# Latent attention scores: two products of 128 rows per head against three of 64, two heads in the two halves of the array

## What is computed

```python
H, DH, LAT = 16, 128, 64
q = (x @ W_q).reshape(B, S, H, DH).transpose(0, 2, 1, 3)
latent = x @ W_kv_down                                    # B, S, 64
kv = (latent @ W_kv_up).reshape(B, S, H, DH).transpose(0, 2, 1, 3)
scores = jnp.einsum('bhqd,bhkd->bhqk', q, kv) / np.sqrt(DH)
probs = jax.nn.softmax(scores, axis=-1)
out = jnp.einsum('bhqk,bhkd->bhqd', probs, kv)
return out.transpose(0, 2, 1, 3).reshape(B, S, H * DH) @ W_o
```

## Time and profile before

| | us |
|---|---|
| time, median of 3 runs | 1693.83 (1692.1 to 1697.16) |
| span of the profiled execution | 1695.7 |
| PE busy over the span | 1441.4 (85%) |
| DVE busy | 1075.4 (63%) |
| ACT busy | 750.3 (44%) |
| POOL busy | 773.8 (46%) |
| all score products (L2131, L2132), busy | 226.5 in 512 records |
| latent attention, first to last score product | 1156.9 to 1539.9 |

### The profile page before, as it was taken

The page is one execution under the profiler, slowest core; times in us unless marked ns, Lnnn a source line. Parts: engine busy times, 40 slices in busy tenths (PEclk is TensorE's granted clock), DMA queues, the critical chain, the costliest instruction groups (busy, mean ns, idle before and its releaser), DMA issues. The chain is left out here.

```text
span 1695.7 us, 39494 instructions
## 1 busy us (share of the span) xinstructions
PE 1441.4 (85%) x14334; PEld 990.9 (58%) x14334; DVE 1075.4 (63%) x2743; ACT 750.3 (44%) x1786; POOL 773.8 (46%) x741
## 2 busy tenths in 40 slices
PE   6879999448889996888999478877899999998799
PEld 3556656414545554455566356654677777777687
DVE  6852222457876564783222388876998888874888
ACT  5533333254555633553333311125776666752322
POOL 4453332763320000454333466606998888973000
PEclk9989999569999998899999788888999999999899
DMA  8309995631110002514999232200000000000000
GB/s 265 98 14 267 284 266 150 204 96 38 38 38 1 1 1 67 152 40 123 280 296 259 73 87 84 78 4 13 3 16 3 12 7 3 16 3 3 10 19 22
DMA packets 92664, 145.50 MB, mean 86 GB/s; under 512 B 25032, under 2 KB 52528, under 8 KB 92512
## 3 DMA queue, kind: packets, MB, share of 16 engines
q1 hardware_dynamic: 62816, 93.06, 19.1%
q0 software_dynamic: 15360, 37.77, 7.7%
q10 hardware_dynamic: 14336, 12.59, 2.7%
HBM read 122.39 MB, written 18.87 MB: 83 GB/s over the span
## 5 line engine op out<-in xcount | busy, mean ns | idle before, releaser
L2298 POOL TENSOR_TENSOR sb_m_prob<-sb_m_prob,sb_m_rinv 128x512 f32<-128x512 f32 x256 | 260.1, 1041 | 44.6 <-DVE sb_m_rinv L2348 40.8
L1272 POOL DMA_INDIRECT sb_c_rows<-slot_rows,sb_slot x192 | 192.1, 1000 | 102.7 <-issue 51.2
L2228 ACT ACTIVATE sb_m_prob<-m_ps_s,sb_m_nmax 128x512 f32<-128x512 f32 x256 | 173.8, 683 | 125.8 <-DVE sb_m_nmax L2354 125.2
L1106 POOL DMA_INDIRECT e_xn<-xn_rows,sb_table x128 | 117.7, 920 | 209.6 <-PE e_ps_x L1184 197.2
L1255 DVE TENSOR_TENSOR sb_e_h<-sb_e_sg,e_ps_gu 96x176 f32<-96x176 f32 x128 | 42.6, 333 | 256.5 <-ACT sb_e_sg L1231 256.5
L1193 PE MATMUL e_ps_gu<-e_wgu,sb_e_xT 128*96 128x352 f32 x512 | 178.1, 470 | 17.0 <-ACT sb_e_xT L1225 15.6
L2354 DVE TENSOR_REDUCE sb_m_nmax<-m_ps_s 128x1 f32<-128x512 f32 x256 | 163.8, 681 | 28.1 <-PE m_ps_s L2132 25.7
L2362 DVE STREAM_TRANSPOSE sb_m_pT<-sb_m_prob 128x1024 f32<-128x1024 f32 x128 | 157.5, 1232 | 0.0
L2145 PE MATMUL m_ps_v<-sb_m_pT,sb_m_lat_rows 32*64 32x128 f32 x8192 | 136.1, 275 | 4.6 <-issue 3.8
L2131 PE MATMUL m_ps_s<-sb_m_latT_high,sb_m_qa 128*128 128x512 f32 x256 | 125.5, 490 | 16.0 <-ACT sb_m_prob L2228 15.9
L2145 PEld LDWEIGHTS m_ps_v<-sb_m_pT,sb_m_lat_rows 32*64 32x64 f32 x8192 | 120.2, 131 | 27.8 <-issue 27.4
(11 more groups left out here) (280 smaller groups left out, 3076.4 us busy)
## 6 DMA issues: line engine op xcount, KB each, us to landing
e_wgu<-wgu SPq DMA_DIRECT2D x128, 352.0 KB, 4.9
e_wdn<-wdn SPq DMA_DIRECT2D x128, 192.0 KB, 4.7
slot_rows<-sb_e_y ACTq DMA_DIRECT2D x128, 96.0 KB
xn_rows<-e_xn SPq DMA_DIRECT2D x16, 256.0 KB, 2.2
sb_c_rows<-slot_rows,sb_slot POOLq DMA_INDIRECT x192, 2.8
sb_x<-x SPq DMA_DIRECT2D x4, 512.0 KB, 5.4
e_xn<-xn_rows,sb_table POOLq DMA_INDIRECT x128, 5.3
sb_g_zm<-wqT SPq DMA_DIRECT2D x1, 2048.0 KB, 9.1
```

Source lines behind the costliest of these rows:

```text
L1106: pool.indirect_dma_start(x, None, k.xn_rows[:, :], bass.IndirectOffsetOnAxis(ap=k.table[:, e:e + 1], axis=0))\
L1272: pool.indirect_dma_start(rows[u][j][:, :], None, k.slot_rows[:, :], bass.IndirectOffsetOnAxis(ap=k.slot[:, n, j:j + 1], axis=0))\
L2228: act.activation(prob[s % 4][:, hh, :], ps_s[j % 3][:, :], ACT.Exp, bias=nmax[s % 2][:, hh:hh + 1], accum_out=rsum[s % 2][:, hh:hh + 1]).t ...
L2298: pool.tensor_tensor(part, part, rinv[s % 2][:, hh:hh + 1].to_broadcast([P, T]), ALU.mult)\
```

## The change

Scores are computed head by head in three products of 64 rows: high x high, low x high, high x low; the product low x low is left out. The queries stay in one layout: `qT` has a high and a low tile of 128 rows, in which the pair's first head has the upper 64 rows and the second the lower 64. The two heads' products alternate, so that neighbours use different halves of the array's rows and different banks.

With this, the wait for the banks is one for both heads at the head of the step; ACT makes one high part of 128 rows for a pair instead of two of 64, in the step after `q_high`; POOL makes one low part instead of two, and no longer waits for its own subtraction before it goes on.

```diff
-        qa = [sb(f"m_qa{u}", [P, 2, T], F32R) for u in range(RING)]
+        qT = [[sb(f"m_qT_{part}{u}", [P, T], F32R) for part in ("high", "low")] for u in range(RING)]
...
             def scores(s):
                 pair, t = s // TB, s % TB
-                b, q = s // PER, qa[pair % RING]
+                b, q = s // PER, qT[pair % RING]
                 if t == 0:
-                    pe.wait_ge(q_ready, 2 * (pair + 1))
+                    pe.wait_ge(q_ready, pair + 1)
                     evicted(pe, ("latT", b))
                 cols = slice(t * P, (t + 1) * P)
-                for hh in range(2):
-                    j = 2 * s + hh
-                    if j >= 3:
-                        pe.wait_ge(p_ready, j - 2)
-                    pe.matmul(ps_s[j % 3][:, :], q[:, hh, cols], latT[b % 2][0][:, :], start=True, stop=False)
-                    pe.matmul(ps_s[j % 3][:, :], q[:, hh, cols], latT[b % 2][1][:, :], start=False, stop=True).then_inc(s_ready, 1)
+                if s:
+                    pe.wait_ge(p_ready, 2 * s - 1)
+                for qpart, lpart in ((0, 0), (1, 0), (0, 1)):
+                    for hh in range(2):
+                        rows = rows_of(hh)
+                        ins = pe.matmul(ps_s[(2 * s + hh) % 3][:, :], q[qpart][rows, cols], latT[b % 2][lpart][rows, :],
+                                        start=(qpart + lpart == 0), stop=(lpart == 1))
+                        if lpart:
+                            ins.then_inc(s_ready, 1)
...
-            def q_part(pair, hh):
-                act.activation(qa[pair % RING][rows_of(hh), hh, :], q_whole[pair % 2][rows_of(hh), :], ACT.Copy)\
-                   .then_inc(high_ready, 1)
+            def q_part(pair):
+                act.activation(qT[pair % RING][0][:, :], q_whole[pair % 2][:, :], ACT.Copy).then_inc(high_ready, 1)
...
-                for back in range(3):
+                for back, part in enumerate((q_high, q_part)):
                     at = misc_of(s - back)
                     if at is not None and at[0] == "q":
-                        if back == 0:
-                            q_high(at[1])
-                        else:
-                            q_part(at[1], back - 1)
+                        part(at[1])
...
-            def q_low(pair, hh):
-                q = qa[pair % RING]
-                pool.wait_ge(high_ready, high_at[("q", pair)] - 1 + hh)
-                pool.tensor_tensor(q[rows_of(1 - hh), hh, :], q_whole[pair % 2][rows_of(hh), :],
-                                   q[rows_of(hh), hh, :].bitcast(F32), ALU.subtract).then_inc(q_ready, 1)
-                pool.wait_ge(q_ready, 2 * pair + hh + 1)
+            def q_low(pair):
+                high, low = qT[pair % RING]
+                pool.wait_ge(high_ready, high_at[("q", pair)])
+                pool.tensor_tensor(low[:, :], q_whole[pair % 2][:, :], high[:, :].bitcast(F32), ALU.subtract).then_inc(q_ready, 1)
...
-                for hh in range(2):
-                    key = misc_of(s - 2 - hh)
-                    if key is not None and key[0] == "q":
-                        pool.wait_ge(scaled, 2 * (s + 1))
-                        q_low(key[1], hh)
+                key = misc_of(s - 2)
+                if key is not None and key[0] == "q":
+                    q_low(key[1])
```

More of the change, by code:

```diff
@@ L2038, in latent_attention @@
     halves = [key for key in uses if key[0] in ("latT", "q")]
-    high_at = {key: sum(1 if x[0] == "latT" else 2 for x in halves[:n + 1]) for n, key in enumerate(halves)}
+    high_at = {key: n + 1 for n, key in enumerate(halves)}
     with ExitStack() as ctx:
@@ L2211, in q_high @@
                 if pair >= 2:
-                    act.wait_ge(q_ready, 2 * (pair - 1))
+                    act.wait_ge(q_ready, pair - 1)
                 act.activation(q_whole[pair % 2][:, :], bank[:, :], ACT.Copy).then_inc(bank_free, 1)
@@ L2242, in _ @@
                 q_high(pair)
-                for hh in range(2):
-                    q_part(pair, hh)
+                q_part(pair)
             def miscellany(s):
                 b, e, key = s // PER, s % PER, misc_of(s)
-                for back in range(3):
+                for back, part in enumerate((q_high, q_part)):
                     at = misc_of(s - back)
                     if at is not None and at[0] == "q":
-                        if back == 0:
-                            q_high(at[1])
-                        else:
-                            q_part(at[1], back - 1)
+                        part(at[1])
                 if b + 1 < B:
@@ L2283, in _ @@
         def _(pool):
-            def q_low(pair, hh):
-                q = qa[pair % RING]
-                pool.wait_ge(high_ready, high_at[("q", pair)] - 1 + hh)
-                pool.tensor_tensor(q[rows_of(1 - hh), hh, :], q_whole[pair % 2][rows_of(hh), :],
-                                   q[rows_of(hh), hh, :].bitcast(F32), ALU.subtract).then_inc(q_ready, 1)
-                pool.wait_ge(q_ready, 2 * pair + hh + 1)
+            def q_low(pair):
+                high, low = qT[pair % RING]
+                pool.wait_ge(high_ready, high_at[("q", pair)])
+                pool.tensor_tensor(low[:, :], q_whole[pair % 2][:, :], high[:, :].bitcast(F32), ALU.subtract).then_inc(q_ready, 1)
             for pair in range(2):
-                for hh in range(2):
-                    q_low(pair, hh)
+                q_low(pair)
             for s in range(NS):
```

## The result

The changed kernel takes 1711.96 us (median of 4 runs, 1704.88 to 1723.8), the kernel before 1692.96 beside it (4 runs, 1691.99 to 1697.16): a ratio of 1.0114, interval 1.0074 to 1.0154. It is slower by 19.0 us. The forecast was 1691.8, with a range of 1684 to 1700; it was wrong, and on the wrong side.

A forecast was written before the change was run, and what follows sets the result against it. PE was taken to set the pace in batches 1 to 3, DVE close behind, DVE and POOL in the first; terms -6.1 + 1.1 + 1.4 - 1.0 + 2.0 + 0.6 = -2.0 on 1693.83 gave 1691.8 us, range 1684 to 1700.

The forecast's parts named there:

- change of tile: Between scores and projection or output product on PE: each switch of 64x128 and 128x128 costs 0.10 us, bounds 0 to 0.11.
- 12 mix cycles: Four-step cycles with an output product, batches 1 to 3: 12.79 us for 13.30, -0.51 each, -6.1 in all.
- six bare cycles: Four-step cycles whose fourth step holds only scores, batches 1 to 3: 11.00 us for 10.81, +0.19 each, +1.1 in all.
- latent cycles: Four cycles in batches 1 and 2 with next batch's latent projections: half of 0.51 us saved each, -1.0 in all.
- first batch: Eight cycles without output product: 1.5 us longer as bare cycles, taken as +2.0 with DVE's other work, bounds -2 and +4.
- The overlap: Score products: both row halves run at once, three rounds of 0.23 us, 0.69 for 0.92 a step.
- second rival: Score rounds: halves do not fully overlap; slower by over 0.3% from 0.25 us a round, 1780 at 0.46; chance 0.10.
- Halves that stand apart in the queue: PE's queue: if the two halves' instructions stood apart, the change would not do what it says; given nothing.
- first rival: Query and mix steps: the half-array tile changes for nothing, another -4.2 us, 1687.6; chance 0.23.
- third rival: Scores after a tile change: second head's weights load after the first's, 0.11 us longer, +11.9, 1703.7; chance 0.08.
- one wait for both banks: Head of each step: all six products wait for the previous step's first exponential, making a loop of 2.55 us a step.
- POOL's relief: Low parts: one instead of two per pair saves some 40 us of POOL, costed at nothing since nobody waits.

The follow-up runs named there:

- added products: Changed kernel plus four half-array products that nobody reads in steps with neither values nor another piece: 1701.54 us, ratio 1.0037.
- heads one after the other: Changed kernel with the first head's three score products queued before the second's three: 1714.11 us in one run.
- own waits: Changed kernel with products ordered head by head and each head waiting for its own bank: 1705.18 us, ratio 1.0068.
- more changes of tile: Kernel before plus one small unread half-array product ahead of each projection and each output product: 1712.66 us, ratio 1.0108.
- both heads on the same half: Changed kernel with both heads' score products on the upper half of the rows: 1814.15 us in one run.

## Why the prediction was wrong

Two steps of the prediction failed. It took a change of tile between 64x128 and 128x128 at 0.10 us, where the runs show 0.21 to 0.22; and it priced all of PE's time at full clock, where the stage ran at half clock for 34 us, which cost 13.3.

Measured at full clock (the run with added products against the kernel before, whose one short stretch at half clock in the first batch is left in; cycles from row maximum to row maximum, as the batches are counted), the terms of the sum came out so:

| | forecast | measured |
|---|---|---|
| 12 mix cycles | -6.1 | +1.2 (159.7 to 160.9) |
| six bare cycles | +1.1 | +2.5 (66.7 to 69.1) |
| latent cycles | -1.0 | +0.1 (47.2 to 47.3) |
| end of the last batch | +1.4 | +1.3 (19.5 to 20.7) |
| first batch | +2.0 | +1.7 (90.4 to 92.1) |
| DVE's work in batches 1 and 2 | +0.6 | within the rows above |
| sum at full clock | -2.0 | +6.7 (383.4 to 390.1) |
| the clock | no term | +13.3 (390.1 to 403.4) |

**The overlap was right.** Rounds of 0.23, as taken. The second rival (halves that do not fully overlap) is out; on one half the products take twice as long. Halves that stand apart in the queue, by which the change might not have done what it says, would not have hurt either, as the run with the heads one after the other shows.

**A change of tile was sized at half its price.** This is the term that turned the mix cycles. The forecast read 0.10 ahead of the values and 0.11 behind them and took each for one change, with 2.02 as the values' own. A change has two parts, 0.10 until the new piece starts and about 0.1 more in it, and with the values one part of each lay inside the 2.02. The values step, where it did not matter, came out at 2.92 to the hundredth; query and mix steps, where it did, 0.2 too long each, 0.4 a cycle, 4.8 on 12 cycles. The rest of the 7.3 lies in the cycles that follow a bare one, where the mix cycle before took only 12.8, and those with latent work. The first rival (the change is free) lay further off still. The third rival had the right price, 0.11 for a load that nothing hides, at the wrong place: the load is not the second head's but the first one of every new piece, and its 11.9 us are near the 8.7 by which the sum at full clock was missed. The Trainium skill's rule, in TensorEngine Tiling (Array Packing), Key Properties, that a switch of the tiling mode drains TensorE, agrees with these runs, where a switch costs 0.21 to 0.22 us.

**The bare cycles lost more, and in part for another reason.** The second one of a batch, the kind that the forecast read, is 0.49 longer where nothing disturbs it, not 0.19. The miss of 0.30 is the query step's changes of tile, 0.2, and the start after the wait, 0.1 (0.14 for 0.05). The reason given for the 0.19, one wait for both banks, holds for 0.1 of a cycle (11.30 to 11.20); the other part is the chain of three products in place of two. On the kernel before the same wait costs 0.52; there the four products behind it run one after the other, while here the heads overlap. The first bare cycle of a batch is not longer at all (11.09 to 11.12 in the second batch, from 1248.16 and from 1252.24), which the forecast did not see.

**What was near by luck.** Three cycles in the table's second and third rows took 0.8 to 1.0 us longer than their like, as one cycle before did. In one of them PE pauses for 0.74 us in the midst of the values, until 1455.77 of the run with added products, and waits for nothing that the profile shows; the cause stays open. These cycles make some 2 of the 6.7, and 0.9 of the +2.5 of the bare cycles. The other +1.6 are near the forecast's +1.1 since three cycles with 0.49 and three with nearly nothing come close to six with 0.19. Without the disturbed ones the latent cycles come to -0.8, near the forecast's -1.0, but as one kind 1.07 shorter (13.01 to 11.94) and another 0.65 longer (10.58 to 11.23), not as half of a mix cycle's gain. The first batch's +1.7 is near its +2.0 too, with single cycles from 0.6 shorter to 0.7 longer, and not by 0.19 in each.

**The clock had no rival.** The forecast priced all of PE's time at full clock, although its first view had a column that said 0.98 for the first batch. Saving PE time where DVE and ACT set the pace leaves PE idle longer, 1.68 us in a row for 0.67, and where that happened with half-array scores the clock went to its lower level. Its 13.3 us are two thirds of the loss. What exactly brings it down stays open. Kernels whose odd steps or all steps use the full array for scores kept 1.00 behind the first batch, even where PE was as idle in a cycle (1.68 of 10.23 us with one product per head, 1.68 of 11.30 with the change). Those with half-array scores in all steps fell there at least once, until more half-array products were added: the changed kernel in every batch, the one with own waits in the second batch alone. The longest wait in a row does not sort them either: with own waits PE waited 0.90 and the clock fell, with full-array products in odd steps it waited 1.45 (ahead of 1359.52) and the clock stayed. All this is from one profile of each, two of the changed kernel.

**Costed at nothing, and nearly right:** POOL's relief, some 1.4 us in the first batch. ACT's was not tested by itself.

## What to carry to other kernels

Two halves of the array at once save a round, but every switch between 64x128 and 128x128 cost nearly as much here as a round of 512 columns, so count the switches before the rounds; in a kernel that interleaves pieces the form pays only where it saves more rounds than it adds switches. When a change leaves PE waiting longer, look at the granted clock of each stretch first and give its fall a rival and a price. And to see whether a loss is the clock, add work that nobody reads: if the clock then holds and the kernel becomes faster, it was.

## What the runs showed of the hardware

- A switch between 64x128 and 128x128 costs 0.21 to 0.22 us (0.89 for four of them with more changes of tile): 0.10 before the new piece and about as much in it.
- Products in different row halves start together even when all three of one half stand ahead of the other's in the queue (heads one after the other: in pairs at 1493.41 and 1493.75). In TensorEngine Tiling (Array Packing), Key Properties, the Trainium skill has tiles work independently of each other; the trace agrees, and shows that the order in the queue does not matter for it here.
- A product of 64 rows takes as long as one of 128, 0.23 us for 512 columns (0.47 for two with both heads on the same half).
- POOL's subtraction takes 1275 ns for 128 partitions, as it did for 64; by line, in the changed kernel:

```profile
L2285 POOL TENSOR_TENSOR sb_m_qT_low<-sb_m_q_whole,sb_m_qT_high 128x512 fp32r<-128x512 f32 x32 | 40.8, 1275 | 49.6 <-ACT sb_m_qT_high L2222 49.6
```

- A stretch at half clock makes the values 3.38 us instead of 2.02, and 34 us of such stretches cost the stage 13.3.
